# Attention over 32 heads: the row maxima beside GpSimd's subtraction, and a quarter of the f16 probabilities converted by GpSimd

## What is computed

```
helical = einsum('bhpsc,bhptc->bhst', qn, kn) / p          # p = 32 pairs
dot     = einsum('bshd,bthd->bhst', qh, kh) / sqrt(hd)     # hd = 16
attn    = softmax(0.5 * dot + 0.5 * helical, axis=-1)
out     = einsum('bhst,bthd->bshd', attn, vh)
```

## Time and profile before

| | |
|---|---|
| three runs | 5821.7 us median (5820.29 to 5823.94) |
| the profiled execution, its own time | 5826.1 us |
| its span, first to last instruction | 5824.3 us |
| mean granted TensorE clock | 0.801 of full speed |
| the stage of the heads, first to last f16 Exp | 3274.6 to 5489.8 us |

### The profile page before, as it was taken

The page is one execution under the profiler, slowest core; times in us unless marked ns, Lnnn a source line. Parts: engine busy times, 40 slices in busy tenths (PEclk is TensorE's granted clock), DMA queues, the critical chain, the costliest instruction groups (busy, mean ns, idle before and its releaser), DMA issues. The chain is left out here.

```text
span 5824.3 us, 66256 instructions
## 1 busy us (share of the span) xinstructions
PE 3447.9 (59%) x14472; PEld 1215.4 (21%) x14472; DVE 4614.3 (79%) x8113; ACT 3031.1 (52%) x3827; POOL 3022.2 (52%) x2350
## 2 busy tenths in 40 slices
PE   8972000000000005879864799999999999999668
PEld 3330000000000002323411132333333333233123
DVE  5464686999999996552677799999999999999452
ACT  5563000000000003542387398989998989899732
POOL 1002465777777772112055266666666666666612
PEclk9986555555555557989977799999999999999889
DMA  1016315232222322000123211111111111110200
GB/s 40 15 35 113 72 16 112 58 65 49 65 56 57 65 49 61 13 11 0 68 107 124 56 32 32 40 39 32 32 33 32 32 32 32 32 37 14 73 32 29
DMA packets 143828, 275.40 MB, mean 47 GB/s; under 512 B 73808, under 2 KB 87504, under 8 KB 136336
## 3 DMA queue, kind: packets, MB, share of 16 engines
q1 hardware_dynamic: 142128, 263.57, 19.2%
q10 hardware_dynamic: 1440, 8.65, 0.4%
HBM read 178.65 MB, written 93.36 MB: 47 GB/s over the span
## 5 line engine op out<-in xcount | busy, mean ns | idle before, releaser
L998 POOL TENSOR_TENSOR att_heads_rest<-att_heads_probs,att_heads_high 128x640 f16<-128x640 f32 x1024 | 1474.4, 1440 | 787.0 <-ACT att_heads_high L1086 781.6
L1116 DVE TENSOR_REDUCE att_heads_maxima<-att_heads_peek 128x1 f32<-128x512 f32 x2048 | 1320.4, 678 | 100.0 <-PE att_heads_peek L1012 96.2
L1084 ACT ACTIVATE att_heads_probs<-att_heads_scores 128x1024 f32<-128x1024 f32 x1024 | 1063.1, 1038 | 262.2 <-PE att_heads_scores L1028 249.5
L1028 PE MATMUL att_heads_scores<-att_heads_q,att_heads_k 128*128 128x512 f16 (+1 forms) x4096 | 1070.6, 383 | 22.7 <-ACT att_heads_high L1086 19.8
L1086 ACT ACTIVATE att_heads_high<-att_heads_scores 128x1024 f16<-128x1024 f32 x1024 | 1063.0, 1038 | 0.0
L1854 PE MATMUL delta_out_sums<-delta_out_squares,main_head_sum 128*128 128x512 f32 x32 | 17.0, 663 | 1762.5 <-ACT delta_out_squares L1883 1762.5
L1136 DVE TENSOR_TENSOR att_heads_rest<-att_heads_probs,att_heads_high 128x384 f16<-128x384 f32 x1024 | 875.2, 855 | 70.9 <-ACT att_heads_high L1086 67.5
L1012 PE MATMUL att_heads_peek<-att_heads_k,att_heads_q 112*128 112x512 f16 x2048 | 808.2, 397 | 151.2 <-DVE att_heads_maxima L1116 70.1
L1733 ACT ACTIVATE delta_scan_s_terms<-delta_scan_state,delta_scan_record 128x64 f32<-128x64 f32 x256 | 104.7, 409 | 1160.5 <-DVE delta_scan_state L1790 1160.5
L1028 PEld LDWEIGHTS att_heads_scores<-att_heads_q,att_heads_k 128*128 128x128 f16 (+1 forms) x4096 | 392.4, 98 | 414.2 <-ACT att_heads_high L1086 53.5
L1044 PE MATMUL att_heads_out<-att_heads_high,att_heads_v_head 128*64 128x512 f16 x2048 | 419.1, 406 | 2.8 <-POOL att_heads_rest L998 2.8
(11 more groups left out here) (226 smaller groups left out, 5438.2 us busy)
## 6 DMA issues: line engine op xcount, KB each, us to landing
delta_scan_record<-delta_record SPq DMA_DIRECT2D x64, 1026.0 KB, 10.5
att_heads_q<-att_hel SPq DMA_DIRECT2D x192, 128.0 KB, 3.1
att_heads_k<-att_hel SPq DMA_DIRECT2D x192, 128.0 KB, 3.2
delta_record<-delta_chunks_record SPq DMA_DIRECT2D x64, 256.5 KB, 4.7
att_hel<-att_hel_high SPq DMA_DIRECT2D x32, 512.0 KB, 3.8
att_hel<-att_hel_rest SPq DMA_DIRECT2D x32, 512.0 KB, 4.3
att_o<-att_heads_out_copy SPq DMA_DIRECT2D x256, 32.0 KB
att_out_parts<-att_o ACTq DMA_DIRECT2D x8, 1024.0 KB, 15.8
```

The source lines that it names most:

```text
L998: nc.gpsimd.tensor_tensor(rest[:, step % 4, SPLIT:], probs[:, step % 4, SPLIT:], high[:, step % 4, SPLIT:], ALU.subtract).then_inc(rest_b_ ...
L1028: mm = nc.tensor.matmul(scores[:, step % 2, tokens(j)], k[0:rows, slot, number, tile * P:(tile + 1) * P], q[0:rows, slot, number, tokens(h ...
L1084: nc.scalar.activation(probs[:, step % 4], scores[:, step % 2], ACT.Exp, scale=LOGIT_SCALE).then_inc(probs_ready, 1)
L1116: nc.vector.tensor_reduce(maxima[:, m:m + 1], peek[:, m % 2], AX.X, ALU.max).then_inc(peek_read, 1)
```

## The change

Four things are changed in `head_attention`:

1. ScalarE's f16 Exp covers columns 0 to 767 (CAST = 768). GpSimd converts the other 256 from `probs`, in a new instruction `cast`, placed behind its subtraction of the step before.
2. SPLIT is 448: VectorE subtracts 448 columns, GpSimd 576. VectorE's subtraction waits for GpSimd's of the same step (`rest_b_ready`).
3. TensorE issues both peeks behind `weigh`, instead of one before `score` and one after.
4. `tile_max` is made behind the maxima of step 23; it is transposed unscaled, into half 0 of `out`, at step 24; the scaling happens where the transposed row is read (step 25). The instruction that wrote `shift` is gone, and no step is without peeks.

```
-        EARLY = 18
+        LAST_PEEKS = 23
+        EARLY = PEEKS - 2 * (LAST_PEEKS + 1)
+        TURN_AT = LAST_PEEKS + 1
+        ROWS_AT = TURN_AT + 1
-        SPLIT = 384
+        SPLIT = 448
+        CAST = 768
...
+                def cast(head, step):
+                    pool.wait_ge(probs_ready, head * STEPS + step + 1)
+                    pool.wait_ge(weighed, head * STEPS + step + 1 + W_CREDIT - 4)
+                    pool.sem_inc(cast_begun, 1)
+                    nc.gpsimd.tensor_copy(high[:, step % 4, CAST:], probs[:, step % 4, CAST:]).then_inc(cast_ready, 1)
...
+                    for step in range(STEPS):
+                        pool.wait_ge(high_ready, head * STEPS + step + 1 + H_CREDIT)
+                        pool.wait_ge(cast_ready, head * STEPS + step + 1)
+                        nc.gpsimd.tensor_tensor(rest[:, step % 4, SPLIT:], probs[:, step % 4, SPLIT:], high[:, step % 4, SPLIT:],
+                                                ALU.subtract).then_inc(rest_b_ready, 1)
+                        if exists(last, slot, 1) or step + 1 < STEPS:
+                            cast(head, step + 1)
...
                 def turn_shifts(quad, slot):
-                    pe.wait_ge(shift_ready, quad * SLOTS + slot + 1)
-                    nc.tensor.transpose(peek[0:QT, 0, 0:P], shift[:], c["identity"][:]).then_inc(shift_turned, 1)
+
+                    pe.wait_ge(max_step, quad * SLOTS + slot + 2)
+                    pe.wait_ge(out_copied, (quad * SLOTS + slot) * 2 + 1)
+                    nc.tensor.transpose(out[0:QT, 0, 0:P], tile_max[:], c["identity"][:]).then_inc(shift_turned, 1)
...
-                        peek_scores(*later(quad, slot, by), peeks[0:1])
                         if step + AHEAD < STEPS:
                             score(quad, slot, step + AHEAD)
                         elif exists(last, slot, 1):
                             score(*later(quad, slot, 1), step + AHEAD - STEPS)
-                        peek_scores(*later(quad, slot, by), peeks[1:2])
-                        weigh(quad, slot, step)
-                        peek_scores(*later(quad, slot, by), peeks[2:])
                         if step == TURN_AT and exists(last, slot, 1):
                             turn_shifts(*later(quad, slot, 1))
+                        weigh(quad, slot, step)
+                        peek_scores(*later(quad, slot, by), peeks)
...
-                    nc.scalar.activation(high[:, step % 4], scores[:, step % 2], ACT.Exp, scale=LOGIT_SCALE).then_inc(high_ready, 1)
+                    nc.scalar.activation(high[:, step % 4, 0:CAST], scores[:, step % 2, 0:CAST], ACT.Exp, scale=LOGIT_SCALE).then_inc(high_ready, 1)
...
-                    nc.vector.tensor_scalar(shift[:], tile_max[:], -LOGIT_SCALE, math.log(PROB_SCALE), ALU.mult, ALU.add).then_inc(shift_ready, 1)
...
-                    nc.vector.tensor_copy(shift_row[:], peek[0:QT, 0, 0:P]).then_inc(shift_row_ready, 1)
+                    nc.vector.tensor_scalar(shift_row[:], out[0:QT, 0, 0:P], -LOGIT_SCALE, math.log(PROB_SCALE), ALU.mult, ALU.add
+                                            ).then_inc(shift_row_ready, 1)
...
                     dve.wait_ge(high_ready, head * STEPS + step + 1 + H_CREDIT)
+                    dve.wait_ge(rest_b_ready, head * STEPS + step + 1 + R_CREDIT)
```

More of the change, by code:

```diff
@@ L881, in head_attention @@
         tile_max = s.sb("tile_max", [P, QT])
-        shift = s.sb("shift", [P, QT])
         shift_row = s.sb("shift_row", [QT, P], F16)
@@ L901, in head_attention @@
         PEEKS = QT * 4
-        TURN_AT = 23
-        EARLY = 18
+        LAST_PEEKS = 23
+        EARLY = PEEKS - 2 * (LAST_PEEKS + 1)
+        TURN_AT = LAST_PEEKS + 1
+        ROWS_AT = TURN_AT + 1
         LOADS = 18 * 16
-        SPLIT = 384
-        PER_QUAD = SLOTS * STEPS
+        SPLIT = 448
+        CAST = 768
         W_CREDIT, H_CREDIT, R_CREDIT, K_CREDIT, O_CREDIT = 2 * STEPS, 4, 4, 2, 2
         def peeks_at(step):
-            if step < TURN_AT:
+            if step <= LAST_PEEKS:
                 return 1, range(EARLY + 2 * step, EARLY + 2 * step + 2)
[L914 to L917, removed]
             return 2, range(2 * (step - TURN_AT), 2 * (step - TURN_AT) + 2)
@@ L990, in _, with turn @@
                 pool.sem_inc(rest_b_ready, R_CREDIT)
-                with pool.Fori(0, QUADS) as quad:
-                    for slot in range(SLOTS):
[L993 to L999, removed]
+                def cast(head, step):
[3 more added lines that the diff above has]
+                    nc.gpsimd.tensor_copy(high[:, step % 4, CAST:], probs[:, step % 4, CAST:]).then_inc(cast_ready, 1)
+                def turn(quad, slot, last):
+                    head = quad * SLOTS + slot
+                    pool.wait_ge(weighed, (head + 1) * STEPS)
+                    nc.gpsimd.tensor_copy(v_head[:, slot, :, 0:V_COLS], v[:, bass.ds(head, 1)].squeeze(1)).then_inc(v_ready, 1)
+                    for step in range(STEPS):
[5 more added lines that the diff above has]
+                            cast(head, step + 1)
+                cast(0, 0)
+                with pool.Fori(0, QUADS - 1) as quad:
+                    for slot in range(SLOTS):
+                        turn(quad, slot, False)
+                for slot in range(SLOTS):
+                    turn(QUADS - 1, slot, True)
             @block.tensor
@@ L1144, in turn @@
                         by, numbers = peeks_at(step)
-                        if step == TURN_AT and exists(last, slot, 1):
-                            shifts(*later(quad, slot, 1))
-                        if step == TURN_AT + 1 and exists(last, slot, 1):
+                        if step == ROWS_AT and exists(last, slot, 1):
                             shift_rows(*later(quad, slot, 1))
@@ L1150, in turn @@
                             read_peeks(*later(quad, slot, by), numbers)
+                        if step == LAST_PEEKS and exists(last, slot, 1):
+                            shifts(*later(quad, slot, 1))
                 for slot in range(SLOTS):
```

6 lines of the change are left out of this document (2 added, 4 removed).

## The result

The changed kernel takes 5858.9 us (median, 5857.1 to 5862.4) against 5821.0 of the kernel before in the same runs. The ratio is 1.0063, 95% interval 1.0051 to 1.0075: slower, by 38 us. The prediction said 5855, with a range of 5725 to 5950.

A forecast was written before the change was run, and what follows sets the result against it. TensorE was taken to bound the kernel at 1.96 us a step, and after the change GpSimd's work plus VectorE's subtraction at 2.11; 58 us more for late heads less 25 for prompt steps gave +33, 5855 us, range 5725 to 5950.

The forecast's parts named there:

- the ring: GpSimd's work and VectorE's subtraction, mutually exclusive, taken one after the other: 1.98 or 2.11 us a step, by their order.
- rule that was weighed: Shared ports held for the whole instruction: about 0.62 instead of 0.36 a step, time near 6120; the prediction decided against it.
- the late step: VectorE's subtraction goes ahead of GpSimd's conversion, whose semaphore wait is uncovered: 1.28 + 0.36 + 0.39 + 0.08 = 2.11 us.
- the prompt step: VectorE's subtraction falls behind GpSimd's conversion, covering GpSimd's wait: 1.98 us; as a rival holding throughout, 5729 us, chance 0.25.
- TensorE's floor: TensorE's ten matmuls fill an ordinary step: 1.96 us, which stays with the peeks together (summed as 1.95).
- the order's course: VectorE starts prompt, falls one step late at the turn and stays so; only the loop boundary's 2.58 restores it, seven times.
- a copy of `out` gives 0.55: Each copy of `out`, twice a head, delays GpSimd by 0.55 us, too little to bring VectorE back.
- the turn: Around the shifts' transpose in each head: TensorE 1.3 us late with the wait for `tile_max`, 1.05 reaching GpSimd.
- the late order: VectorE one step late, subtracting ahead of GpSimd's conversion: 2.11 us a step, 70.3 a head; chance 0.63.
- The need for about 0.8: GpSimd would have to be late by about 0.8 us for VectorE to get back to prompt.
- the sum: Heads at 70.3 against 68.5: 58 us more over 32 heads, less 25 for prompt steps in eight heads: +33 us.
- the chain over three steps: Second bound in the late order, f16 Exp through subtractions, `weigh`, peeks, scores to Exp: 6.12 over three steps, 2.04 us.

The follow-up runs named there:

- e3: The kernel before plus GpSimd's conversion of 256 columns (f16 Exp cut to 768), nothing else: 5959.8 us, ratio 1.0235 to the kernel before.
- e9: The changed kernel with 384 columns converted by GpSimd instead of 256: 6022.1 us, ratio 1.0334 to the kernel before.
- e12: The kernel before with the new handling of `tile_max`, SPLIT 512, 128 columns converted, peeks apart, no VectorE wait: 5724.9 us, ratio 0.9828 to the kernel before.
- e1: The changed kernel without the conversion, ScalarE making all 1024 f16 columns again: 5812.6 us, ratio 0.9981 to the kernel before.
- e2: The changed kernel without VectorE's wait for GpSimd's subtraction of the same step: 5855.5 us, ratio 1.0051 to the kernel before.
- e5: e4 with both peeks behind `weigh`; SPLIT 384, no wait, no conversion: 5818.2 us, ratio 0.9989 to the kernel before.
- e4: The kernel before with only the new handling of `tile_max` (transposed unscaled at step 24, scaled when read): 5712.2 us, ratio 0.9805 to the kernel before.
- e6: e4 with SPLIT 448 and VectorE's wait for GpSimd's subtraction, peeks apart, no conversion: 5776.1 us, ratio 0.9918 to the kernel before.
- e7: The changed kernel with the peeks apart, one ahead of the scores and one behind: 5835.4 us, ratio 1.0021 to the kernel before.
- e10: e4 with SPLIT 448 and no VectorE wait: 5710.2 us, ratio 0.9803 to the kernel before.
- e11: e4 with VectorE's wait for GpSimd's subtraction of the same step, SPLIT 384: 5788.7 us, ratio 0.9932 to the kernel before.
- e8: The changed kernel with GpSimd's conversion two steps ahead instead of one: 5950.2 us, ratio 1.0215 to the kernel before.

## Why the prediction came out as it did

The time was 4 us off, and that is in part luck: the path to it had errors of both signs.

**Right: ScalarE and idle GpSimd were not what to relieve.** e3 shows that the conversion alone costs 135 us, e9 that more of it is worse.

**Right: the terms of the ring.** Conversion 0.39 predicted, 0.387 measured alone, and with e9 and e12 0.82 ns a column plus 0.18. GpSimd's subtraction 1.28, measured 1.28. VectorE 0.48 behind, measured 0.47. What GpSimd loses behind VectorE 0.36, measured 0.77 - 0.39 = 0.38, though VectorE's subtraction takes 0.61 where it starts alone (3887.28). By the Trainium skill's rule that was weighed (SBUF — State Buffer, section SBUF: two separate sides), the pair is held for the whole instruction. Here the two exclude each other, but what the second loses, 0.38, is less than the first one's 0.61.

**Mis-sized: the late step.** 2.11 predicted, 2.17 measured. GpSimd's wait for its own conversion is 0.16, not the 0.08 of the earlier trace rows.

**Right by luck: the prompt step.** 1.98 predicted, 1.96 measured, from other terms. GpSimd's wait for its own conversion was taken as covered, and is 0.15 here too (3889.36 to 3889.51); the subtraction loses 0.19 and not 0.36, as it waits out a part of VectorE's in that time. TensorE's floor comes to the same 1.96, so these rows don't tell which of the two binds.

**Failed: the order's course, "VectorE starts prompt" and "a copy of `out` gives 0.55. Only the loop boundary with its 2.58 does".** Counted over all 1024 steps of the changed kernel, from the end of GpSimd's subtraction to VectorE's start for the same step, VectorE is late (1.3 us or more) in 702, prompt (under 0.15) in 253, and between the two in 69. At each turn it goes from prompt to late over steps 25 to 27, as predicted. But the turn isn't needed for it: in the first head VectorE is late from step 3 on, long before a turn. The same count gives 644 late steps in e1, 696 in e2, 683 in e5 and 980 in e9, all with the peeks together, and 4 to 41 in e3, e4, e6, e7, e10, e11 and e12, with the peeks apart. Only e8, together but with the conversion moved, has 22. So the late order needs the grouped peeks, and comes without the conversion too; the prediction looked for its cause at the turn. The step above 1.96 doesn't need it: e3, where no wait holds VectorE back, has its 2.22 with VectorE in time, queued ahead of the conversion.

Nor did the prediction see how VectorE comes back. The loop boundary doesn't restore it: behind one, only step 0 is prompt. The middle copy of `out` does, in every head: GpSimd idled 1.10 for the f32 Exp behind it (3886.78), and VectorE's subtraction, at 3887.28, was 0.05 ahead of GpSimd's next. It stays prompt from step 18 until the turn. At a head's end it doesn't come back. GpSimd's timeline:

```profile
3915.86 0.64 POOL L998 COPY att_heads_v_head<-att_v 128x528 f16 x1
3916.47 1.27 POOL L1002 TENSOR_TENSOR att_heads_rest<-att_heads_probs,att_heads_high 128x576 f16<-128x576 f32 x1
...
3920.69 0.40 POOL L993 CAST att_heads_high<-att_heads_probs 128x256 f16<-128x256 f32 x1 [0.79 <-ACT att_heads_probs L1096]
3921.24 1.28 POOL L1002 TENSOR_TENSOR att_heads_rest<-att_heads_probs,att_heads_high 128x576 f16<-128x576 f32 x1
```

and VectorE's:

```profile
3921.50 1.49 DVE L1148 TENSOR_TENSOR att_heads_rest<-att_heads_probs,att_heads_high 128x448 f16<-128x448 f32 x1
```

GpSimd's copy of the values stands before it, only 0.79 of idle is left, and VectorE is 0.26 behind GpSimd's start.

In both places VectorE comes 1.60 behind the end of GpSimd's last subtraction; GpSimd's next one starts 1.65 behind that end in the middle and 1.34 at a head's end. The need for about 0.8 was sized rightly (the step must grow from 2.17 by 0.71). What failed is the 0.55 for a copy of `out`: at the middle one the step is 2.93, 0.76 more. In an ordinary head VectorE is late for 23 of 32 steps (0 to 17 and 27 to 31), where I had 32 in all but eight heads.

**How the errors add up.** In the profiled executions the stage grew by 25.5 us, where the sum said 33. An ordinary head was to be 70.3 and is 69.3. It can be written as 18 steps at 2.17 and 14 at 1.96, with 0.84 + 0.62 for the copies and 1.07 + 0.39 for the turn on top. Against the prediction that is +1.0 for the late step's 0.06, -2.1 for the fourteen steps at 1.96, -0.2 for the copies (1.69 predicted) and +0.4 for the turn (1.05 predicted): -0.9 a head. Every fourth head is 0.25 longer, so the mean is about -0.8, and -26 over 32 heads. The 25 us that the prediction took off for prompt steps in eight heads are contained in this, so they come back: +25. The first head and the loop boundaries cost 10 less than before, where I had left them as they were: -10. The last two heads, with few or no peeks in them, grew by 5.8 instead of 1.9: +4. Together about -7, as the stage shows. Some 7 us behind the stage, which the sum doesn't contain, bring the difference of the profiled spans to 32; that of the medians is 38. That this lies so near to 33 is luck.

**Near in the changed kernel, wrong in general: the turn.** 1.05 predicted; measured 1.07 for the step (3.03 against 1.96) and 0.39 for a later one (2.35), with TensorE idle 0.80 where "about 1" was said. But I took the wait for `tile_max` as a property of the new turn. e4 has the same turn for 0.1: it is the grouped peeks that make the last maxima late.

**Failed: "TensorE: the same ten matmuls, the peeks together: ... its floor of 1.96 stays. So ScalarE's shorter Exp and VectorE's moved wait can't make an ordinary step faster."** That a floor stays doesn't say that it binds. Grouped peeks cost 106 us (e5) and the wait 76 (e11) where there is no conversion; I had costed both at nothing in an ordinary step; a TensorE that loses more to waits for maxima stood only among the signs of being wrong, without a price. The pattern of three fits the chain over three steps that I had named, at 2.04, as a second bound of the late order only: Exp, GpSimd's subtraction, VectorE's, `weigh`, scores, Exp. In e1 it comes to (1.96 + 1.96 + 2.41) / 3 = 2.11, in e11 to 2.01. In the changed kernel's late steps the ring, at 2.17, is longer than it and hides it, which fits e2, where the wait is worth nothing. So the wrong step did little to the sum, and the range, 225 us wide, could hold the rest. Neither is to the credit of the reasoning: the parts were never priced alone, so it couldn't show that the turn alone is worth 112 us, or that grouped peeks take 106 of them.

**Open.** How e7's third step of 2.41 is shared between ring and chain isn't settled, and e7 without VectorE's wait was not run. Nor is it settled what the uncovered 0.16 is worth, since e8 made a new wait.

## What to carry to other kernels

Idle time on an engine is not room, if its work excludes another engine's: add up what two engines do one after the other, and compare that with the step. When a change has several parts, time each alone: here the turn alone is worth 2%, and the parts put beside it took it all back. A bound from matmul counts is only a floor; the order of small instructions that fill a two-place buffer decides whether it is reached. Before calling an order of two engines a property of one part, count it in every kernel: here the order that seemed to belong to the conversion and the turn came with the grouped peeks.

## What the runs showed of the hardware

- GpSimd's conversion f32 to f16 takes 0.282, 0.387 and 0.493 us for 128, 256 and 384 columns: this one-input GpSimd instruction costs 0.82 ns a column, the two-input subtraction 1.9 (1.16, 1.28 and 1.40 for 512, 576 and 640).
- Who was there first decides, to some hundredths: VectorE's subtraction 0.05 ahead of GpSimd's went first (3887.28 and 3887.33), and 0.26 behind GpSimd's it went after it (3921.24 and 3921.50). The late order then keeps itself to step 17. The Trainium skill (SBUF — State Buffer, section Who interferes with whom) says that the order of issue decides which engine blocks; these rows agree.
- GpSimd, waiting for its own last instruction, starts 0.15 to 0.16 behind its end (4001.22 and 4001.38), where two of its instructions without a wait overlap by 0.04 (4000.49 and 4000.45).
